# A mixture-of-experts kernel: a small chunk's sums move to another PSUM bank, its gates are made later, and the gathered additions get a second rate

## The chip, the cores and the metric

The kernel runs on one core of one Trainium2 chip. The metric is the device time of one execution in microseconds (us), median over the runs. Within the core five engines run side by side, each with its own instruction stream and held together by semaphores: PE (TensorE, matmuls and weight loads), DVE (VectorE), ACT (ScalarE), POOL (GpSimd) and SP (SyncE, which here only issues DMAs).

## What is computed

x has 2 x 1024 rows of 256 values, all in float32. `xn` is x with its rows normalised.

```python
s = group_norm(tanh(relu(rope(xn @ W_Q)) + hh_b)), turned per batch     # the branch
idx, w = top 6 of 32 experts for each row (within the best 4 of 8 groups of experts)
moe    = sum over the 6 experts: w * (relu(xn @ W1[e].T) ** 2) @ W2[e].T
shared = (relu(xn @ Ws1.T) ** 2) @ Ws2.T
out = x + s * silu(shared + moe)
```

## The kernel before, in words

The 2048 rows are 16 tiles of 128 rows, in four chunks of four tiles. `DENSE = (4, 1, 0, 0)` (line 32) splits them in two kinds. The four tiles of chunk 0 and one tile (number 4) of chunk 1 are *dense*: every one of the 32 experts is computed for all of their rows, and the row's gate (zero where the expert was not chosen) multiplies the hidden values. `BLOCKS` is the list of these two chunks, 0 and 1. The other 11 tiles are *routed*: their rows are sorted by expert into 97 tiles of slots, each slot tile goes through one expert, its results are stored in the table `ytab`, and each row then collects its six results.

The work is a list of 74 units, k = 0 to 73 (`units()`, line 84):

- k = 0 to 7, the early units: the shared experts of all chunks.
- k = 8 to 17: the first ten dense units of chunk 0, one expert over four tiles each.
- k = 18 to 42: the 25 groups of slots, up to four slot tiles each. `LAST` is 42.
- k = 43 to 64: the other 22 dense units of chunk 0.
- k = 65 to 73: the nine dense units of chunk 1. Unit 65 holds the two shared experts of tile 4, each of the other eight holds four experts for that one tile.

Each engine walks the same counter k in program order, and what it does at a k is written out by hand. For a dense unit:

- PE, `first(k)` (lines 951 to 953): the first layer into the bank `hp[k % 2]`; it waits until DVE has read unit k - 2 out of that bank. Then, at the same k, `second_dense(k - 2)` (line 990): the second layer of the unit before last, added up in PSUM over all experts.
- DVE, `relu(k)` (line 1246; line 1248 where there is no gate), then the additions of this k, then `finish` (lines 1273 and 1276) for an output tile that is due.
- ACT, `square(k)` (line 680), later `leave_sum` (line 715), which copies the finished sums out of PSUM at k = 67 for chunk 0 and k = 76 for chunk 1, and `silu_sum` (line 726).
- SP loads the gates of a unit, spread over all partitions, from a table in HBM (`load_gate`, line 471), three units ahead.

PSUM has eight banks: two for `hp`, three for `rot` (turned slot tiles and results of slots, dealt out in turn by the list `uses`, lines 412 to 435), two for `dp`, one for `bp`. Both chunks add up their dense sums in `dp`. So the first `second_dense` of chunk 1, `second_dense(65)` at k = 67, waits for the semaphore `sum_out`, which ACT raises when it has copied chunk 0's sums out, and ACT does that at k = 67 behind `square(67)`.

The additions: from k = 46 (`ADD_AT`) DVE adds the 11 x 6 = 66 gathered pieces, number 0 to 65, to their rows (`add`, line 1265). POOL issues one indirect DMA for each (line 623), in order, at most five ahead of the additions (`AHEAD`, `yk_used`). `adds_by(k)` says how many additions are done by the end of k; with `ADDS = (12, 5)` it grows by 2.4 for each unit:

```python
adds_by = lambda k: max(0, min(NR * K, ADDS[0] * (k - ADD_AT + 1) // ADDS[1]))
```

At k = 65 to 73 these are 3, 2, 2, 3, 2, 3, 2, 2, 2 additions. Output tiles are finished in the order of `FINISH`: tile 12 at k = 66, tiles 0 to 3 at 68 to 71, tiles 13, 14, 15 at 72 to 74 and tile 4 at 77; DVE's part of it stands one k later.

The start of the slots: `one_hot(i)` on DVE (lines 1283 and 1285), `rows_hot(i)` on ACT (line 685) and `place` on PE (line 900) build, routed tile by routed tile (i = 0 to 10), the table of which row stands in which slot. They are laced between the units k = 8 to 14. When all are done DVE writes `ids` (line 1356), and POOL starts the 97 gathers of x (line 614), at most eight ahead of PE, which turns them (`turn_slots`, line 915).

The gates of a dense chunk: `weigh(c)` on DVE (lines 1141 to 1156) normalises the weights and makes a seed for a root; `gate_root(b)` on POOL (lines 580 to 588, 13 instructions for three Newton steps) takes the root; `turn_gates(b)` on PE (line 863) turns the gates; `copy_gates(b)` on ACT (line 670) copies them out; `store_gates(b)` on SP (line 463) stores them and waits until they have landed. For chunk 1 before: `weigh(1)` behind `one_hot(1)`, `gate_root(1)` on POOL between two `low_w` steps (line 569, the low halves of the first-layer weights), and the rest at k = 14 and 15.

Of the kernel before, what the change touches and what calls it, by code (L numbers as in the profile page):

```python
# [6 lines left out]
ACT = mybir.ActivationFunctionType  # L7
# [14 lines left out]
KG, K = 4, 6  # L22
NT = B * T // P
J = 4
NCH = NT // J
# [6 lines left out]
DENSE = (4, 1, 0, 0)  # L32
BLOCKS = [c for c in range(NCH) if DENSE[c]]
# [4 lines left out]
NR = len(ROUTED)  # L38
# [10 lines left out]
GROUPS = (TILES + J - 1) // J  # L49
# [6 lines left out]
POOL_STEPS = 11  # L56
# [6 lines left out]
HRING = 4  # L63
# [3 lines left out]
OHRING = 4  # L67
GRING = 3
LEAD = 10
ADDS = (12, 5)  # L70

W_SCALE = 64.0
WQ_SCALE = 256.0
# [21 lines left out]
def build(nc, x, w1, w2, wr, br, wq, hh_b, gn, cos, sin, consts, out, xtab, ytab, gtab):  # L95
    with ExitStack() as ctx:
# [3 lines left out]
        def bank(name, shape, dt=F32):  # L100
            return ctx.enter_context(nc.psum_tensor(name, shape, dt))
# [12 lines left out]
        w2s = sb("w2s", [P, N, D])  # L114


        acc = xs
# [101 lines left out]
        hf = sb("hf", [P, HRING, CH])  # L219
# [3 lines left out]
        rot = bank("rot", [P, 3, 2, D])  # L223
        dp = bank("dp", [P, 2, 2, D])
        bp = bank("bp", [P, 2, D])
        flat = lambda b: rot[:, b].rearrange("p a d -> p (a d)")
        turned_x = lambda b: flat(b).bitcast(F16).rearrange("p (h k t r) -> p h k t r", h=2, k=KC, t=2)
        turned_words = lambda b: rot[:, b].rearrange("p t (k r) -> p t k r", r=P)
# [11 lines left out]
        gt_stored = sem("gt_stored")  # L240
# [23 lines left out]
        gt_ready = sem("gt_ready")  # L264
# [18 lines left out]
        xt_copied = sem("xt_copied")  # L283
# [5 lines left out]
        shared_out = sem("shared_out")  # L289
# [3 lines left out]
        sum_out = sem("sum_out")  # L293
# [12 lines left out]
        UNITS, EARLY = units()  # L306
        NU = len(UNITS)
        unit_at = {u: k for k, u in enumerate(UNITS)}
# [10 lines left out]
        leaves = {}  # L319
# [8 lines left out]
        store_no = {kh: v for v, kh in enumerate(slot_exits)}  # L328
# [3 lines left out]
        shared_no = {kh: v for v, kh in enumerate(kh for kh in exits if kh not in store_no)}  # L332
        sums = [(c, h) for c in BLOCKS for h in range(len(pairs_of(dense_tiles(c))))]
# [5 lines left out]
        PLACE_AT = HOT_AT + 1  # L339
        HOT_PAIRS = pairs_of(range(NR))  # L340
        PLACED = PLACE_AT + len(HOT_PAIRS)
        GATES_AT = [4, PLACED - 1][0:len(BLOCKS)]


        FIRST_SLOTS = EARLY + LEAD
# [14 lines left out]

        LAST = unit_at[("slots", GROUPS - 1, 0)]
        ADD_AT = LAST + 4
        adds_by = lambda k: max(0, min(NR * K, ADDS[0] * (k - ADD_AT + 1) // ADDS[1]))

        def sums_at(j):

# [35 lines left out]
        def wait_y(engine, v):  # L402
            if exit_by_act(*slot_exits[v]):
                engine.wait_ge(y_act, y_act_before(v + 1))
            else:
                engine.wait_ge(y_out, v + 1 - y_act_before(v + 1))
# [5 lines left out]
        uses = []  # L412
        for k in range(NU + 2):
# [3 lines left out]
            if k + 2 in leaves and UNITS[k + 2][0] == "slots":  # L417
                uses.append(("turn", k + 2, 0))
            uses += [("leave", i, h) for i in leaving(k) for h in range(i != LAST, len(leaves[i]))]
        use_no = {use: n for n, use in enumerate(uses)}  # L420
        bank_of = {use: n % 3 for n, use in enumerate(uses)}

        def wait_bank(engine, *use):

            n = use_no[use]
            if n < 3:
                engine.wait_ge(shared_out, len(shared_no))
                engine.wait_ge(eoff_ready, 1)
                engine.wait_ge(gt_ready, len(BLOCKS))
            else:  # L430
                what, k, h = uses[n - 3]
                if what == "turn":
                    engine.wait_ge(xt_copied, leaves[k][h][-1] + 1)
                else:
                    wait_y(engine, store_no[k, h])

        @block.sync
        def _(sp):
# [111 lines left out]
        def _(pool):  # L550
# [52 lines left out]
            gate_root(0)  # L603
            for s in range(1, POOL_STEPS):
                low_w(s)
                if s == POOL_STEPS - 3:
                    for b in range(1, len(BLOCKS)):
                        gate_root(b)
            pool.wait_ge(ids_ready, 1)
            pool.wait_ge(xtab_stored, 16 * len(ROUTED_CHUNKS))  # L610
            for a in range(TILES):
                if a >= XRING:
                    pool.wait_ge(t_done, a - XRING + 1)
                nc.gpsimd.indirect_dma_start(xg[:, a % XRING, :], None, xtab,  # L614
                                             bass.IndirectOffsetOnAxis(ids[:, a:a + 1], 0))\
                  .then_inc(xg_landed[a % XRING], 16)
            for s in range(YRING):
                pool.wait_ge(y_stored[s], 16 * len(range(s, len(slot_exits), YRING)))
            pool.wait_ge(wlo_dve, WSTEPS - POOL_STEPS)
# [8 lines left out]
        def _(act):  # L628
# [83 lines left out]
            def leave_sum(c):  # L712
                act.wait_ge(sum_done, BLOCKS.index(c) + 1)
                for h, own in enumerate(pairs_of(dense_tiles(c))):
                    nc.scalar.activation(acc[:, own[0]:own[-1] + 1, :], dp[:, h, 0:len(own), :], ACT.Copy)\
                      .then_inc(sum_out, 1)

            def silu_sum(j):
                f = FINISH.index(j)
                if j in ROUTED:  # L720
                    act.wait_ge(yk_used, K * (ROUTED.index(j) + 1))
                else:
                    act.wait_ge(sum_out, 1 + sums.index((j // J, j % J // 2)))
                if f >= 2:
                    act.wait_ge(rows_ready, f - 1)
                nc.scalar.activation(tz[:, f % 2, :], acc[:, j, :], ACT.Silu).then_inc(tz_ready, 1)

            def leave_shared_of(k):
# [97 lines left out]
        def _(pe):  # L826
# [28 lines left out]
            def turn_gates(b):  # L855

                pe.wait_ge(groot_ready, b + 1)
                if b == 0:
                    pe.wait_ge(th_ready, NCH)
                else:  # L860
                    pe.wait_ge(shared_out, len(shared_no))
                for q in range(DENSE[BLOCKS[b]]):
                    mm = nc.tensor.transpose((flat_q, flat(0))[b][0:E, q * P:(q + 1) * P], root[:, q, :], ident)
                mm.then_inc(gt_turned, 1)
# [114 lines left out]
            def second_dense(k):  # L979
                kind, c, u = UNITS[k]  # L980
                pe.wait_ge(squared, k + 1)
                if u == 0 and c != BLOCKS[0]:
                    pe.wait_ge(sum_out, sum(1 for i, h in sums if i < c))
                for n in range(experts_in(c, u)):
                    e = u + n
                    pe.wait_ge(w2_landed[e // W2STEP], 16)
                    for q in range(DENSE[c]):

                        cols = slice((n * DENSE[c] + q) * P, (n * DENSE[c] + q + 1) * P)
                        mm = nc.tensor.matmul(dp[:, q // 2, q % 2, :], hf[:, k % HRING, cols], w2s[:, e, :],  # L990
                                              start=(e == 0 and q % 2 == 0), stop=(e == N - 1), skip_group_check=True)
                if k == last_of[c]:
                    mm.then_inc(sum_done, 1)
# [83 lines left out]
        def _(dve):  # L1077
# [266 lines left out]
            for i in range(NR):  # L1344
                one_hot(i)
                if i % 2 == 1 or i == NR - 1:
                    relu(HOT_AT + i // 2)
                if i == 1:
                    weigh(1)

            dve.wait_ge(one_used, NR)

# [10 lines left out]
            for k in range(HOT_AT + len(HOT_PAIRS), END):  # L1363
# [8 lines left out]
                for s in range(POOL_STEPS, WSTEPS):  # L1372
                    if k == PLACED - 1 + (s - POOL_STEPS) // 2:
                        low_w(s)
                for c in range(2, NCH):
                    if k == WEIGH_AT(c):
                        weigh(c)
                for i in range(0, NR, 2):
# [71 lines left out]
```

## Time and profile before

| | us |
|---|---|
| median of 3 runs | 336.25 |
| the three runs | 336.25, 334.22, 1024.59 |
| the profiled execution, its own time | 335.13 |
| its span, first to last instruction | 333.3 |
| PE busy | 297.5 (89%) |
| DVE busy | 229.0 (69%) |
| ACT busy | 179.3 (54%) |
| POOL busy | 208.0 (62%) |
| mean granted TensorE clock | 0.968 |

All times in rows are microseconds from the first instruction of the profiled execution; 1.83 us of its time lie outside of the span. Busy shares are means over stages with different limits, so what a change in one stage is worth is to be read from that stage. The first views are the page's 40 slices of 8.3 us, for where an engine pauses, and then the chain of waits and the timelines around those pauses.

### The profile page before, as it was taken

The page shows a single profiled execution, that of the slowest core. Times are in us where ns is not written, and L with a number is a line of the kernel's source. Part 1 is how long each engine was busy: PE and PEld are TensorE (multiplying, and loading weights), DVE is VectorE, ACT ScalarE, POOL GpSimd, SP SyncE. Part 2 cuts the span into 40 slices and gives each one's busy share as a digit, 9 for nine tenths or more (in the row PEclk, how much of TensorE's full clock was granted, in tenths as well). Part 3 has the DMA queues.
Part 4 walks back from the last instruction along what each step waited for, and adds up shares of the span by engine and source line. Part 5 has one row for each costly group of instructions (what it writes and reads, how often), then busy time and mean ns, then how long its engine had stood idle before and what let it go on. Part 6 is the DMA issues. An engine that isn't in the chain of part 4 may idle for free.

```text
span 333.3 us, 6927 instructions
## 1 busy us (share of the span) xinstructions
PE 297.5 (89%) x2224; PEld 231.8 (70%) x2224; DVE 229.0 (69%) x585; ACT 179.3 (54%) x293; POOL 208.0 (62%) x226
## 2 busy tenths in 40 slices
PE   0577899879997999999999999998999999995994
PEld 0344666547776977888888698885767767785893
DVE  3788678887631378677778767687767576753774
ACT  3888598695452755557665576653363331212322
POOL 1874656681577777777777777304666777774640
PEclk9997899989997999999999999999999999995999
DMA  7455746722463376676766767555688777666552
GB/s 283 188 176 190 239 146 244 283 94 63 104 180 116 108 222 204 201 204 207 219 203 194 219 196 210 183 173 192 181 327 259 220 197 212 189 182 163 147 154 79
DMA packets 39651, 62.92 MB, mean 189 GB/s; under 512 B 5282, under 2 KB 25538, under 8 KB 39618
## 3 DMA queue, kind: packets, MB, share of 16 engines
q1 hardware_dynamic: 31794, 41.11, 37.2%
q0 software_dynamic: 7824, 21.38, 23.4%
q8 instruction: 20, 0.33, 0.4%
q14 instruction: 13, 0.11, 0.1%
HBM read 46.13 MB, written 16.33 MB: 187 GB/s over the span
## 4 chain that ended last, share of the span: by engine, by line
PE 56%; DMA 15%; POOL 8%; DVE 7%; ACT 6%; issue 6%; DVEq 1%; ACTq 0%
PE rot L962 12%; PE dp L990 10%; DMA yk<-ytab,slot 10%; PE rot L915 5%; PE hp L939 4%; DMA xgt<-xtab,ids 4%; POOL xgt L614 4%; PE hp L951 3%; PE hp L953 3%; PE hp L952 3%; POOL yk L623 3%; PE hp L941 3%; PE hp L940 3%; PE rot L975 2%; DVE xs L1265 2%
## 5 line engine op out<-in xcount | busy, mean ns | idle before, releaser
L614 POOL DMA_INDIRECT xgt<-xtab,ids x97 | 96.4, 994 | 39.7 <-issue 21.3
L680 ACT ACTIVATE hf<-hf 128x512 f32<-128x512 f32 (+2 forms) x74 | 45.8, 619 | 98.7 <-DVE hf L1246 74.8
L623 POOL DMA_INDIRECT yk<-ytab,slot x66 | 64.7, 980 | 44.3 <-DMA ytab<-late 17.1
L990 PE MATMUL dp<-w2s,hf 128*128 128x256 f32 x340 | 83.6, 391 | 4.3 <-issue 4.3
L990 PEld LDWEIGHTS dp<-w2s,hf 128*128 128x128 f32 x340 | 66.1, 198 | 16.2 <-issue 4.7
L694 ACT ACTIVATE xgt<-rot 128x1024 f16<-128x1024 f16 (+1 forms) x49 | 49.3, 1009 | 9.6 <-PE rot L915 9.2
L962 PE MATMUL rot<-w2s,hf 128*128 x194 | 51.3, 391 | 1.1 <-ACT xgt L694 1.0
L953 PE MATMUL hp<-xh,wlo 128*128 128x512 f16 (+2 forms) x148 | 45.0, 322 | 0.0
L952 PE MATMUL hp<-xh,whi 128*128 128x512 f16 (+2 forms) x148 | 45.0, 322 | 0.0
L951 PE MATMUL hp<-xh,whi 128*128 128x512 f16 (+2 forms) x148 | 44.9, 321 | 0.0
L1265 DVE SCALAR_TENSOR_TENSOR xs<-yk,wk,xs 128x256 f32<-128x256 f32 x66 | 32.0, 484 | 16.8 <-DMA yk<-ytab,slot 14.8
L1246 DVE SCALAR_TENSOR_TENSOR hf<-hp,gate_bc 128x512 f32<-128x512 f32 x40 | 27.6, 689 | 20.0 <-PE hp L953 18.4
L939 PE MATMUL hp<-xgt,whi 128*128 128x128 f16 x194 | 38.3, 224 | 1.7 <-issue 1.6
L941 PE MATMUL hp<-xgt,wlo 128*128 128x128 f16 x194 | 37.9, 221 | 0.0
L962 PEld LDWEIGHTS rot<-w2s,hf 128*128 128x128 f32 x194 | 33.3, 190 | 6.5 <-issue 1.9
L940 PE MATMUL hp<-xgt,whi 128*128 128x128 f16 x194 | 37.8, 221 | 0.0
L1248 DVE TENSOR_SCALAR hf<-hp 128x512 f32<-128x512 f32 (+2 forms) x26 | 17.2, 663 | 24.7 <-PE hp L941 22.5
L1258 DVE COPY late<-rot 128x512 f32<-128x512 f32 (+1 forms) x37 | 25.2, 683 | 12.5 <-PE rot L962 12.3
L915 PE MATMUL rot<-cst,xgt 128*128 128x128 f32 x194 | 29.4, 274 | 1.5 <-DMA xgt<-xtab,ids 1.4
L915 PEld LDWEIGHTS rot<-cst,xgt 128*128 128x128 f32 x194 | 23.7, 141 | 6.2 <-DMA xgt<-xtab,ids 2.2
L939 PEld LDWEIGHTS hp<-xgt,whi 128*128 x194 | 18.9, 98 | 6.6 <-issue 3.0
L953 PEld LDWEIGHTS hp<-xh,wlo 128*128 128x128 f16 x148 | 15.3, 103 | 10.4 <-issue 2.0
(162 smaller groups left out, 473.5 us busy)
## 6 DMA issues: line engine op xcount, KB each, us to landing
ytab<-late SPq DMA_DIRECT2D x48, 256.0 KB, 2.8
gate_bc<-gtab SPq DMA_DIRECT2D x40, 256.0 KB, 3.8
late<-in_w SPq DMA_DIRECT2D x17, 256.0 KB, 4.9
w2s<-in_w SPq DMA_DIRECT2D x8, 512.0 KB, 6.4
xs<-in_x SPq DMA_DIRECT2D x4, 512.0 KB, 4.7
xgt<-in_x SPq DMA_DIRECT2D x4, 512.0 KB, 6.5
out<-xgt SPq DMA_DIRECT2D x16, 128.0 KB, 3.7
xgt<-xtab,ids POOLq DMA_INDIRECT x97, 3.3
```

Of the source, the lines that this page charges most:

```text
L614: nc.gpsimd.indirect_dma_start(xg[:, a % XRING, :], None, xtab, bass.IndirectOffsetOnAxis(ids[:, a:a + 1], 0))\
L623: nc.gpsimd.indirect_dma_start(yk[:, n % KRING, :], None, ytab, bass.IndirectOffsetOnAxis(slot[:, n // K, n % K:n % K + 1], 0))\
L694: nc.scalar.activation(xt[:, at:at + len(own), :, :, :].rearrange("p a k h r -> p (a k) h r"), halves(bank_of["turn", k, h])[:, 0:len(own) ...
L915: mm = nc.tensor.transpose(turned_words(bank_of["turn", k, h])[:, q, kc, :], xg[:, a % XRING, kc * P:(kc + 1) * P], ident)
L939: nc.tensor.matmul(o, hi, xt[:, a % TRING, kc, HIGH, :], start=(kc == 0), stop=False)
L940: nc.tensor.matmul(o, hi, xt[:, a % TRING, kc, LOW, :], start=False, stop=False)
L941: mm = nc.tensor.matmul(o, lo, xt[:, a % TRING, kc, HIGH, :], start=False, stop=(kc == KC - 1))
L951: nc.tensor.matmul(o, hi, xh[:, 0, kc, cols], start=(kc == 0), stop=False)
L952: nc.tensor.matmul(o, hi, xh[:, 1, kc, cols], start=False, stop=False)
L953: mm = nc.tensor.matmul(o, lo, xh[:, 0, kc, cols], start=False, stop=(kc == KC - 1))
L962: mm = nc.tensor.matmul(rot[:, bank_of["leave", k, h], q, :], hf[:, k % HRING, s * P:(s + 1) * P], w2_all[:, bass.ds(at[k][s], D)], start= ...
L990: mm = nc.tensor.matmul(dp[:, q // 2, q % 2, :], hf[:, k % HRING, cols], w2s[:, e, :], start=(e == 0 and q % 2 == 0), stop=(e == N - 1), s ...
```

## The change

- `ADDS = (48, 55, 20)`: the additions grow by 48/20 = 2.4 for each unit up to `SECOND` = 65, and by 55/20 = 2.75 for each unit from there. At k = 65 to 73 they are 3, 3, 2, 3, 3, 3, 2, 2, 0.
- Chunk 1's sums are added up in `rot` (bank 0, since it has one tile) in place of `dp`. `second_dense(65)` no longer waits for `sum_out`; it waits until chunk 1's gates are ready and the last user of bank 0 in the list of slots (the result of slot group 23) has been copied out.
- `weigh(1)` goes from behind `one_hot(1)` to k = 20, in the slots.
- `gate_root(1)` goes from between POOL's weight steps to behind its 97 gathers of x.
- `GATES_AT[1]` goes from 14 to 45: `turn_gates(1)` and `copy_gates(1)` run at k = 45, `store_gates(1)` at k = 46.
- The waits of the first three users of `rot` ask for the gates of chunk 0 alone. The first `silu_sum` waits until both gate tables are stored, since their source shares its memory with `tz`.

```diff
-ADDS = (12, 5)
+ADDS = (48, 55, 20)
...
+        sums_of = lambda c: dp if c == BLOCKS[0] else rot
...
-        GATES_AT = [4, PLACED - 1][0:len(BLOCKS)]
+        GATES_AT = [4, EARLY + LEAD + GROUPS + 2][0:len(BLOCKS)]
...
-        adds_by = lambda k: max(0, min(NR * K, ADDS[0] * (k - ADD_AT + 1) // ADDS[1]))
+        SECOND = unit_at[("dense", BLOCKS[1], 0)]
+        adds_by = lambda k: max(0, min(NR * K, (ADDS[0] * (min(k + 1, SECOND) - ADD_AT)
+                                                + ADDS[1] * max(0, k + 1 - SECOND)) // ADDS[2]))
...
+        def wait_left(engine, use):
+            what, k, h = use
+            if what == "turn":
+                engine.wait_ge(xt_copied, leaves[k][h][-1] + 1)
+            else:
+                wait_y(engine, store_no[k, h])
 
         def wait_bank(engine, *use):
...
-                engine.wait_ge(gt_ready, len(BLOCKS))
...
+                engine.wait_ge(gt_ready, 1)
...
             for s in range(1, POOL_STEPS):
                 low_w(s)
-                if s == POOL_STEPS - 3:
-                    for b in range(1, len(BLOCKS)):
-                        gate_root(b)
...
+            for b in range(1, len(BLOCKS)):
+                gate_root(b)
             for s in range(YRING):
                 pool.wait_ge(y_stored[s], 16 * len(range(s, len(slot_exits), YRING)))
...
             def leave_sum(c):
...
-                    nc.scalar.activation(acc[:, own[0]:own[-1] + 1, :], dp[:, h, 0:len(own), :], ACT.Copy)\
+                    nc.scalar.activation(acc[:, own[0]:own[-1] + 1, :], sums_of(c)[:, h, 0:len(own), :], ACT.Copy)\
...
             def silu_sum(j):
...
+                elif f == 0:
+                    act.wait_ge(gt_stored, 16 * len(BLOCKS))
...
             def turn_gates(b):
...
-                    pe.wait_ge(shared_out, len(shared_no))
+                    wait_left(pe, last_user[0])
...
             def second_dense(k):
...
                 if u == 0 and c != BLOCKS[0]:
-                    pe.wait_ge(sum_out, sum(1 for i, h in sums if i < c))
+                    pe.wait_ge(gt_ready, len(BLOCKS))
+                    for b in range(-(-DENSE[c] // 2)):
+                        wait_left(pe, last_user[b])
...
-                        mm = nc.tensor.matmul(dp[:, q // 2, q % 2, :], hf[:, k % HRING, cols], w2s[:, e, :],
+                        mm = nc.tensor.matmul(sums_of(c)[:, q // 2, q % 2, :], hf[:, k % HRING, cols], w2s[:, e, :],
...
             for i in range(NR):
                 one_hot(i)
                 if i % 2 == 1 or i == NR - 1:
                     relu(HOT_AT + i // 2)
-                if i == 1:
-                    weigh(1)
...
-                for c in range(2, NCH):
+                for c in range(1, NCH):
                     if k == WEIGH_AT(c):
                         weigh(c)
```

## Rows read from the trace of the kernel before

**Rows 1.** The page's busy share in tenths, 40 slices of the span: PE and POOL.
```profile
PE   0577899879997999999999999998999999995994
...
POOL 1874656681577777777777777304666777774640
```

**Rows 2.** Timeline of PE, 296 to 304 us: start, duration, line, operation, idle before.
```profile
296.00 1.95 PE L990 MATMUL dp<-w2s,hf 128*128 128x256 f32 x8
297.78 0.22 PE L951 MATMUL hp<-xh,whi 128*128 128x128 f16 x1
...
299.07 0.22 PE L953 MATMUL hp<-xh,wlo 128*128 128x128 f16 x1
303.59 2.05 PE L990 MATMUL dp<-w2s,hf 128*128 128x256 f32 x4 [4.30 <-issue]
```

**Rows 3.** Windows: stretch, busy PE, PEld, DVE, ACT, POOL; then PEclk, DMA share, GB/s.
```profile
299.30:303.60 4.30, 0.01 (x1) 0.04 (x1) 3.36 (x8) 2.54 (x5) 3.38 (x4) 0.75 0.77 180
303.60:308.00 4.40, 4.40 (x29) 3.85 (x29) 0.37 (x1) 0.00 (x0) 1.31 (x2) 0.50 0.51 154
```

**Rows 4.** Timeline of ACT, 300 to 334 us: the two leave_sum.
```profile
302.42 1.07 ACT L715 ACTIVATE xs<-dp 128x512 f32<-128x512 f32 x2
...
329.17 0.38 ACT L715 ACTIVATE xs<-dp 128x256 f32<-128x256 f32 x1 [1.80 <-PE dp L990]
```

**Rows 5.** Timeline of POOL: gathers number 56, 57 and 65 of y.
```profile
304.27 0.95 POOL L623 DMA_INDIRECT yk<-ytab,slot  x1 [0.30 <-issue]
309.59 1.13 POOL L623 DMA_INDIRECT yk<-ytab,slot  x1 [4.37 <-DVE xs L1265]
...
320.01 0.94 POOL L623 DMA_INDIRECT yk<-ytab,slot  x1 [0.30 <-DVE xs L1265]
```

**Rows 6.** The tile yk, 285 to 334 us: from a gather's issue to its landing.
```profile
DMA to landing us min/median/max: 3.1/4.1/5.2
```

**Rows 7.** Timeline of DVE in chunk 1's units: relu(66); a finish and relu(71).
```profile
298.99 0.69 DVE L1246 SCALAR_TENSOR_TENSOR hf<-hp,gate_bc 128x512 f32<-128x512 f32 x1
...
316.97 0.43 DVE L1273 TENSOR_TENSOR xs<-tz,rows 128x256 f32<-128x256 f32 x1 [0.16 <-issue]
...
317.81 0.69 DVE L1246 SCALAR_TENSOR_TENSOR hf<-hp,gate_bc 128x512 f32<-128x512 f32 x1
```

**Rows 8.** Timeline of DVE, 60 to 64 us: weigh(1) starts, then one_hot(2).
```profile
60.04 0.29 DVE L1141 TENSOR_REDUCE wsum<-gate 128x4 f32<-128x128 f32 x1
...
61.61 0.95 DVE L1283 TENSOR_TENSOR xgt<-iota,fb 128x768 f16<-128x768 f16 x1
62.48 1.73 DVE L1285 TENSOR_TENSOR xgt<-iota,fa 128x588 f16<-128x588 f16 x1
```

**Rows 9.** Timeline of ACT at 67 us: the copy of chunk 3's shared sums.
```profile
67.12 1.06 ACT L701 ACTIVATE xs<-rot 128x512 f32<-128x512 f32 x2
```

**Rows 10.** Timeline of PE, 66 to 73 us: place of routed tiles 3 and 4.
```profile
66.75 0.44 PE L900 MATMUL bp<-xgt 128*128 128x98 f16 x6 [0.82 <-ACT xgt L685]
...
71.86 0.44 PE L900 MATMUL bp<-xgt 128*128 128x98 f16 x6 [1.65 <-ACT xgt L685]
```

**Rows 11.** Windows, columns as in rows 3: behind those pauses, and inside the slots.
```profile
72.80:75.50 2.70, 2.70 (x11) 1.23 (x9) 0.71 (x1) 2.07 (x4) 2.56 (x4) 0.50 0.02 4
...
131.20:161.20 30.00, 29.13 (x266) 25.21 (x267) 21.69 (x43) 19.91 (x28) 22.96 (x24) 1.00 0.71 210
```

**Rows 12.** Timeline of POOL: low_w, gate_root(1)'s last, first gathers of x and y.
```profile
62.22 1.35 POOL L569 TENSOR_TENSOR wlo<-late,whi 128x512 f16<-128x512 f32 x1 [2.40 <-ACT whi L654]
...
73.03 0.60 POOL L588 TENSOR_TENSOR eq<-gate,gseed 128x32 f32<-128x32 f32 x1
...
86.18 1.58 POOL L614 DMA_INDIRECT xgt<-xtab,ids  x1 [10.34 <-DVE ids L1356]
...
229.04 1.10 POOL L623 DMA_INDIRECT yk<-ytab,slot  x1 [17.06 <-DMA ytab<-late]
```

**Rows 13.** DMA issues: chunk 1's gate store, KB, us to landing.
```profile
gtab<-tz SPq DMA_DIRECT2D x1, 16.0 KB, 3.5
```

More of the change, by code:

```diff
@@ L419, in build @@
             uses += [("leave", i, h) for i in leaving(k) for h in range(i != LAST, len(leaves[i]))]
-        use_no = {use: n for n, use in enumerate(uses)}
-        bank_of = {use: n % 3 for n, use in enumerate(uses)}
+        bank_of, user_before, last_user = {}, {}, {}
+        for n, use in enumerate(uses):
+            bank_of[use], user_before[use], last_user[n % 3] = n % 3, last_user.get(n % 3), use
+        def wait_left(engine, use):
[4 more added lines that the diff above has]
+                wait_y(engine, store_no[k, h])
         def wait_bank(engine, *use):
-            n = use_no[use]
-            if n < 3:
+            if user_before[use]:
+                wait_left(engine, user_before[use])
+            else:
                 engine.wait_ge(shared_out, len(shared_no))
                 engine.wait_ge(eoff_ready, 1)
-                engine.wait_ge(gt_ready, len(BLOCKS))
[L430 to L435, printed above, removed]
+                engine.wait_ge(gt_ready, 1)
         @block.sync
```

## The prediction

> **What bounds the kernel now.** I read the page's 40 slices first [rows 1]. PE stands at 9 tenths from the tenth slice on, with few exceptions. The last is slice 37 (300 to 308 us), a 5 between nines. POOL is at a steady 7 in the slots and again from slice 32 on, where it gathers y. A gather is about 0.95 us busy and 0.30 us idle, so 7 tenths of busy time is POOL without a pause. Two engines are near their limit, and a stall that goes from one may find the other.
>
> The timeline of PE opens the dip [rows 2]. PE ends `first(67)` at 299.12 and starts `second_dense(65)` only at 303.59, idle 4.30 us. The row names no releaser, but the code has one wait there, `sum_out`. ACT's copy of chunk 0's sums runs from 302.42 to 303.49 [rows 4], and PE starts 0.1 us after it. The copy stands behind `square(67)`, that behind `relu(67)`, that behind the additions of k = 66: a wait for a PSUM bank has tied PE to DVE's additions. The pause costs more than itself. [...]
>
> After that PE runs unbroken until ACT takes chunk 1's sum at 329.17 [rows 4]. From there to the end of the span are 4.13 us (copy, silu, two DVE instructions, one store), which the change leaves as they are.
>
> **The change, part 1: another bank for chunk 1's sums.** `second_dense(65)` can start at 299.12; its new conditions, chunk 1's gates and bank 0 free, are met some 60 us earlier. PE's own work from there is: `second_dense(65)` half of 1.78 us = 0.89; six `first` (68 to 73) at 299.12 - 297.78 = 1.34 us; eight `second_dense` (66 to 73) at 297.78 - 296.00 = 1.78 us [rows 2]. Together 0.89 + 8.04 + 14.24 = 23.2 us, so PE alone would end at 322.3 instead of 329.17: 6.9 us less, 4.5 from the pause and 2.4 from the clock.
>
> I don't think that the rest of the core lets it. What is late next are the additions. In the kernel before, POOL issues gather 56 at 304.27, then stands still for 4.37 us because DVE is stuck behind PE, and issues gathers 57 to 65 from 309.59 to 320.01: 10.42 us for eight steps, 1.30 each [rows 5]. At its shortest a step is 0.95 + 0.30 = 1.25. I take 1.28. Without the pause gather 65 starts at 304.27 + 9 x 1.28 = 315.8. It ends its issue 0.95 us later and lands 4.1 us after that (3.1 to 5.2 [rows 6]), at 320.85.
>
> **Part 2: the new rate.** It adds no work; it moves additions forward. The last two stand at k = 72, ahead of `relu(73)`, no longer behind it. A unit with three additions needs 3 x 1.28 = 3.84 us of gathers, and PE's unit takes 1.34 + 1.78 = 3.12 us. DVE is already late: `relu(66)` runs at 298.99 [rows 7], though PE had ended that first layer near 296.0 [rows 2]. PE tolerates a relu that starts up to about 4.2 us after the end of its `first` (two `second_dense` and a `first`, 4.9, less relu's 0.69). Walking the units with these numbers, an addition never earlier than its gather's landing: relu(67) starts at 302.2, relu(68) at 305.8 (4.2 late, just in time), relu(69) at 308.8, relu(70) at 313.5. PE is free for `first(72)` at 312.7 and waits 1.4 us for relu(70), then some 0.7 us for relu(71).
>
> The end follows from the last gather. Add 65 starts at 320.85 and ends at 321.35; `finish` of tile 3 takes 0.16 + 0.84 = 1.00 (316.97 to 317.81 [rows 7] and the idle before); `relu(73)` 0.69, to 323.05; square 0.63, to 323.7; `second_dense(73)` 1.78, to 325.5. Then the 4.13 us: 329.6 against 333.3, a gain of 3.7 us. The bounds are 6.9 (PE alone decides) and about 1.0: landing at its longest, 1.1 later, and the new pauses dropping the clock in two units, 1.6 more. ACT does its copy of chunk 0 at the same place, beside PE now, and costs nothing.
>
> **Part 3: weigh(1) off the path of `ids`.** `weigh(1)` takes DVE from 60.04 to 61.61, 1.57 us, ahead of one_hot(2) [rows 8]. Here DVE is on the chain. ACT scales what one_hot makes, and PE waits for ACT twice, 0.82 us for tile 3 and 1.65 us for tile 4 [rows 10]; between the two ACT works without a pause. Then PE is unbroken until `place` ends, DVE writes `ids`, and POOL, idle for 10.34 us, starts the gathers of x at 86.18 [rows 12]. So an earlier DVE comes out at the gathers nearly whole. What can swallow some is ACT's copy of the shared sums, since it needs PE's result, which the timeline has ready near 65.7; the copy's two halves start at 67.12 [rows 9], so up to about 1.9 us there is room. I take 1.7 us: the 1.57, and 0.1 from the transpose and copy of chunk 1's gates, which also leave k = 14.
>
> From `ids` on everything moves along. In the slots PE is busy 29.13 of 30 us, and POOL shows 22.96 of 30, gathers back to back [rows 11]; both start earlier by the same amount. [...] I expect pauses of about 1.3 us in place of 2.5, and leave the clock as it is.
>
> The 1.73 us row starts while POOL is inside its `low_w` (62.22 to 63.57 [rows 12]) and ends soon after it. [...]
>
> weigh(1) at k = 20 puts 1.6 us on DVE in the slots, whose relu there has some 4 us of slack: nothing.
>
> **Part 4: gate_root(1), and what goes with it.** On POOL it lasts from 63.57 to 73.63, 10.1 us. Its absence there gives nothing, since POOL then waits 10.34 us for `ids` anyway [rows 12]. Behind the gathers of x it falls into the 17.06 us in which POOL waits for the last y store (211.98 to 229.04): 7 us of cover are left. PE asks for it at k = 45, at about 232. SP's `store_gates` at k = 46 holds SP for its landing, about 3.5 us [rows 13]; queued behind it are one gate load per unit, needed three units (over 9 us) later, and the reloads of x, needed from k = 50. Cost nothing; without cover 3 us. The new wait of the first silu is past by then.
>
> **Sum.** The profiled execution took 335.13 us. 335.13 - 3.7 - 1.7 = 329.7. The median shown, 336.25, stands 1.1 above that execution, and its lowest run 0.9 below.
>
> **Rivals.**
> - *PE alone sets the end.* Gathers land early and DVE keeps up: 335.13 - 6.9 - 1.7 = 326.5. For it: landings down to 3.1 us. Against it: POOL's step cannot go below 1.25, and DVE is 2.7 us late when chunk 1 starts. 0.12.
> - *The clock comes back at the start.* [...] For it: shorter pauses. Against it: they are still over 1 us. 0.13.
> - *Most of it is given back.* [...] 0.23.
> - *Slower: the clock stays low in chunk 1.* [...] At that clock four matmuls of `second_dense` took 1.84 us (303.59 to 305.43) in place of 0.89, and a `first` doubles too, so a unit costs 3.1 us more. The savings of PE's work and of the start are 6.9 + 1.7 = 8.6, so it decides from the third such unit; with five it is 335.13 - 8.6 + 15.6 = 342.1. For it: pauses of 2.5 and 4.3 us dropped the clock here. Against it: it was back within about 4.4 us both times [rows 3, 11], and the pauses I expect are shorter. 0.05.
>
> **How the numbers follow.** The forecast has 0.47, and its own range is 328.4 to 331.6. The range 326.3 to 333.6 leaves out the slower rival, part of the given-back case and a little of the first. Two per cent, about what a measurement of this kernel can tell from no change, is 6.7 us, so faster begins at 328.4. The first two rivals give 0.25 between them, less a little of the second, and the forecast's lower edge adds some: 0.31. Slower: 0.05. The rest, 0.64, is within 2%, though I expect most of it below the time before.
>
> **What would show it.** Right: PE's pause at 299 is gone, and `second_dense(65)` follows `first(67)` at once; POOL has no pause over 1 us from gather 50 to 65; DVE waits for yk in k = 68 to 72, and PE shows one or two pauses of about 1 us late in chunk 1; last matmul about 3.7 us earlier relative to the first y gather. The first gather of x starts near 84.5, the first of y near 227.3. POOL's gate_root stands near 211 with idle time behind it. [...]

## The result, and the profile after

| | before | after |
|---|---|---|
| median (20 runs each), us | 335.83 | 331.83 |
| lowest run, us | 334.19 | 328.21 |
| profiled execution, us | 335.13 | 328.21 |
| its span, us | 333.3 | 326.4 |

The ratio after / before is 0.9861, with a 95% interval of 0.9835 to 0.9886: some 4 us faster, and inside of 2%. Here and below medians are over all runs, while ratios leave out the slow ones, those more than 1.5% above the fastest of their kernel. The forecast was 329.7 with a range of 326.3 to 333.6. The profiled execution of after is the lowest of its 20, so differences between the two profiles (6.9 us) are larger than those between the medians (4.0 us), and what follows keeps the two apart.

The page's slices for after, to be held against [rows 1] (copies at other line numbers: `relu` is L1257, `add` L1276, `second_dense` L1001, `leave_sum` L722):

```profile
PE   0578889989989989999999999998999999999793
...
POOL 1874755430777777777777777333666777777730
...
PEclk9998999999999999999999999999999999999998
```

The 5 of PE in slice 37 is gone; a 7 in slice 38 holds what is left of it. POOL gathers at a steady 7 to slice 38. Its 6, 8, 1 in slices 8 to 10 have become 4, 3, 0 (gate_root(1) gone), and its 3, 0, 4 in slices 26 to 28 have become 3, 3, 3 (gate_root(1) come).

PE in chunk 1 has four short pauses, 3.26 us together, in place of the one of 4.30 us [rows 2]. The timeline of PE, start, duration, what ran, idle before:

```profile
302.80 0.23 PE L960 MATMUL hp<-xh,whi 128*128 128x128 f16 x1 [0.77 <-DVE hf L1257]
...
310.29 0.23 PE L960 MATMUL hp<-xh,whi 128*128 128x128 f16 x1 [1.07 <-DVE hf L1257]
...
317.40 1.99 PE L1001 MATMUL rot<-w2s,hf 128*128 128x256 f32 x8 [0.58 <-ACT hf L687]
...
320.23 1.99 PE L1001 MATMUL rot<-w2s,hf 128*128 128x256 f32 x8 [0.84 <-ACT hf L687]
```

The first two wait for a `relu`, as the forecast had it: `first(70)` for relu(68) and `first(72)` for relu(70). The last two stand in front of the last two `second_dense` and wait for ACT's square, which stands behind relu(72) and relu(73). None of the four drops the clock: it reads 1.00 behind each. The windows of the same stretches, columns as in [rows 3]:

```profile
299.00:303.60 4.60, 3.83 (x46) 3.27 (x44) 2.71 (x6) 1.50 (x4) 3.37 (x5) 1.00 0.61 163
303.60:308.00 4.40, 4.40 (x49) 4.02 (x47) 2.16 (x5) 1.05 (x3) 3.49 (x4) 1.00 0.76 202
72.80:75.50 2.70, 2.70 (x24) 1.89 (x23) 2.70 (x5) 2.28 (x4) 0.00 (x0) 1.00 0.29 95
```

Where [rows 3] had 0.50, behind the pause of 4.30 us, there is 1.00, and it stays 1.00 to PE's last matmul. The third window shows the same for the stretch behind `place` [rows 11], where I had left the clock at 0.50.

The chain of waits at the end names the new bound. Of its last steps these two are gathers, with start, time until landed, and what moved:

```profile
303.44 4.60 DMA yk<-ytab,slot
312.34 4.98 DMA yk<-ytab,slot
```

and DVE's timeline shows what is behind that last landing:

```profile
316.71 1.12 DVE L1276 SCALAR_TENSOR_TENSOR xs<-yk,wk,xs 128x256 f32<-128x256 f32 x2
317.99 0.43 DVE L1284 TENSOR_TENSOR xs<-tz,rows 128x256 f32<-128x256 f32 x1 [0.16 <-issue]
318.49 0.42 DVE L1287 TENSOR_TENSOR xgt<-xs,xgt 128x256 f32<-128x256 f32 x1
318.83 0.68 DVE L1257 SCALAR_TENSOR_TENSOR hf<-hp,gate_bc 128x512 f32<-128x512 f32 x1
```

The last gather (312.34, issue 0.94) lands at 317.3. Its addition, a finish and `relu(73)` follow, and PE's last eight matmuls start at 320.23, after an idle 0.84 us. ACT takes the sum at 322.26.

Cut at events that both kernels have, the two profiles differ as follows. x0 is the first gather of x, y0, y56 and y65 the gathers of y with these numbers, leave is `leave_sum` of chunk 1 (each from the timelines; differences worked out).

| stretch, us | before | after | difference |
|---|---|---|---|
| start to relu(8) | 59.25 | 58.92 | -0.33 |
| relu(8) to x0 | 26.93 | 23.27 | -3.66 |
| x0 to y0 (slots) | 142.86 | 142.43 | -0.43 |
| y0 to y56 | 75.23 | 76.19 | +0.96 |
| y56 to y65 | 15.74 | 11.53 | -4.21 |
| y65 to leave | 9.16 | 9.92 | +0.76 |

The last two rows together, y56 to leave, are 24.90 and 21.45 us, 3.45 less.

### The profile page after: what moved, and what is told of

Its sections match the earlier page's. It is cut to its first block, busy times and chain, and to the rows that moved or that the text cites. A ratio compares the mean times of both kernels' runs of the same rounds, so it can differ in the third digit from the quotient of the medians.

```text
span 326.4 us, 6929 instructions
## 1 busy us (share of the span) xinstructions
PE 293.6 (90%) x2224; PEld 227.7 (70%) x2224; DVE 228.0 (70%) x585; ACT 178.4 (55%) x293; POOL 204.2 (63%) x226
## 4 chain that ended last, share of the span: by engine, by line
PE 46%; DMA 16%; POOL 13%; DVE 9%; issue 7%; ACT 7%; DVEq 2%; ACTq 0%; POOLq 0%
PE rot L971 12%; DMA yk<-ytab,slot 12%; POOL yk L630 7%; POOL xgt L619 5%; PE rot L924 5%; PE dp L1001 4%; PE hp L948 4%; PE hp L950 3%; DMA xgt<-xtab,ids 3%; PE hp L949 3%; PE hp L962 2%; PE hp L961 2%; PE hp L960 2%; PE rot L984 2%; DVE xs L1276 2%
## 5 line engine op out<-in xcount | busy, mean ns | idle before, releaser
L630 POOL DMA_INDIRECT yk<-ytab,slot x66 | 65.9, 999 | 26.9 <-issue 14.3
L1001 PE MATMUL dp<-w2s,hf 128*128 128x256 f32 x272 | 64.9, 381 | 0.0
L1001 PEld LDWEIGHTS dp<-w2s,hf 128*128 128x128 f32 x272 | 51.8, 192 | 9.6 <-issue 0.2
L1276 DVE SCALAR_TENSOR_TENSOR xs<-yk,wk,xs 128x256 f32<-128x256 f32 x66 | 31.9, 484 | 21.1 <-DMA yk<-ytab,slot 18.8
L960 PE MATMUL hp<-xh,whi 128*128 128x512 f16 (+2 forms) x148 | 42.8, 310 | 1.8 <-DVE hf L1257 1.8
L962 PE MATMUL hp<-xh,wlo 128*128 128x512 f16 (+2 forms) x148 | 43.1, 312 | 0.0
L961 PE MATMUL hp<-xh,whi 128*128 128x512 f16 (+2 forms) x148 | 43.1, 311 | 0.0
L1257 DVE SCALAR_TENSOR_TENSOR hf<-hp,gate_bc 128x512 f32<-128x512 f32 x40 | 27.5, 687 | 12.9 <-PE hp L962 12.0
L577 POOL TENSOR_TENSOR wlo<-late,whi 128x512 f16<-128x512 f32 x11 | 16.3, 1485 | 14.5 <-ACT whi L661 14.4
```

The costliest lines, as they stand in the source:

```text
L630: nc.gpsimd.indirect_dma_start(yk[:, n % KRING, :], None, ytab, bass.IndirectOffsetOnAxis(slot[:, n // K, n % K:n % K + 1], 0))\
L960: nc.tensor.matmul(o, hi, xh[:, 0, kc, cols], start=(kc == 0), stop=False)
L961: nc.tensor.matmul(o, hi, xh[:, 1, kc, cols], start=False, stop=False)
L962: mm = nc.tensor.matmul(o, lo, xh[:, 0, kc, cols], start=False, stop=(kc == KC - 1))
L1001: mm = nc.tensor.matmul(sums_of(c)[:, q // 2, q % 2, :], hf[:, k % HRING, cols], w2s[:, e, :], start=(e == 0 and q % 2 == 0), stop=(e == N ...
```

## The experiments

There are twelve entries for nine kernels (d1, d2 and d3 repeat c1, c3 and a4), measured in three batches: the four a; then b1, b2, c1, c3; then b3, d1, d2, d3. Each batch ran on a chip of its own, with runs of the kernel before beside it (medians 335.78, 335.66 and 371.58). All ratios are to the before of the same batch. After itself is in none of them; its ratio is that of the result. Edits are given against after.

### The bank and the rate, taken apart

a1 keeps the bank alone; a2 adds the new rate; a3 is the late weigh(1) and gates alone; a4 is after with the old rate.

```diff
-ADDS = (48, 55, 20)
+ADDS = (48, 48, 20)          # a1, a3, a4
...
-        GATES_AT = [4, EARLY + LEAD + GROUPS + 2][0:len(BLOCKS)]
+        GATES_AT = [4, PLACED - 1][0:len(BLOCKS)]     # a1, a2, with weigh(1) and gate_root(1) at their old places
...
-        sums_of = lambda c: dp if c == BLOCKS[0] else rot
+        sums_of = lambda c: dp                         # a3, with the wait for sum_out
```

> The changed kernel with the start as before (weigh(1) behind one_hot(1), gate_root(1) between the weight steps, gates at k = 14) and the additions at 2.4 a unit throughout: only the sums' bank is new. Theory A (the last gather sets chunk 1's end, and how many additions stand ahead of relu(73) decides what it costs): PE's pause of 4.3 us goes; with two additions behind relu(73) that relu waits for gather 63 and not 65, so the tail gains more than the 3.7 us of the prediction, about 6 (ratio 0.982), and DVE is late by under 3 us at k = 68 to 70. Rival B (the bank frees PE, but the additions at the old rate then pile up behind the units and cost what they save): 2 to 3 us (0.992). x gathers start near 86 in both.

> The changed kernel with the start as before: bank and new rate of additions, nothing of the start. The prediction's tail: 3.7 us less than before (ratio 0.989). Theory A: slower than the same kernel at the old rate by 1 to 2.6 us, since relu(69) to relu(73) wait for gathers that land at 3.84 us a unit where PE needs 3.12. Rival B: faster than the old rate by 1 us or more.

> The changed kernel with both chunks' sums in dp and the wait for sum_out as before, additions at 2.4 a unit: only weigh(1), gate_root(1) and the gates' turning are moved. Theory A: x gathers start 1.7 us earlier (84.5) where the clock still drops near 70 us, 4.0 earlier (82.2) where it does not, as in the profile of the changed kernel; in the median 2 to 3 us (ratio 0.992). Rival C (the start's gain is lost in the slots, where PE and POOL are both full): ratio 0.998 to 1.000 with the x gathers early all the same. PE's pause of 4.3 us near 295 stays.

> The changed kernel with the additions at 2.4 a unit throughout (48, 48, 20), all else as changed. Theory A: no pause of PE in chunk 1, relu(73) waits for gather 63; 1 to 2.5 us faster than the changed kernel (ratio 0.980 against 0.986). Rival B (the new rate is worth its place: additions left behind the last unit lengthen the end): 1 us or more slower than the changed kernel (0.989).

| | median, us (runs) | ratio, 95% | PE's pauses in chunk 1 | y65 to leave | y56 to leave |
|---|---|---|---|---|---|
| a1 | 329.91 (6) | 0.982, 0.9769 to 0.9871 | 0.16, 0.31, 0.93 | 7.23 | 18.80 |
| a2 | 334.42 (12) | 0.9954, 0.992 to 0.9987 | 1.16, 0.46, 0.66 | 9.56 | 21.22 |
| a3 | 334.30 (6) | none given | 4.29 | 9.16 | 24.33 |
| a4 | 328.42 (6) | 0.9768, 0.9719 to 0.9818 | none | 6.57 | 18.40 |

The bank is worth 5.9 us when nothing else is changed (a1, 6 expected), and PE's pause of 4.3 us stays where the sums stay in `dp` (a3). a3's median says little: its six runs go from 327.86 to 337.22. The new rate costs: 4.5 us from a1 to a2, where 1 to 2.6 were expected, and 3.4 us from a4 to after. In both pairs the intervals don't touch, and a1 and a2 are of one batch. a2 also holds the forecast's tail alone, and gave 1.4 us in the median where 3.7 (ratio 0.989) was expected. a4's DVE shows why the rate costs:

```profile
317.26 0.43 DVE L1284 TENSOR_TENSOR xs<-tz,rows 128x256 f32<-128x256 f32 x1 [0.16 <-ACT tz L735]
317.76 0.42 DVE L1287 TENSOR_TENSOR xgt<-xs,xgt 128x256 f32<-128x256 f32 x1
318.11 0.68 DVE L1257 SCALAR_TENSOR_TENSOR hf<-hp,gate_bc 128x512 f32<-128x512 f32 x1
318.71 1.05 DVE L1276 SCALAR_TENSOR_TENSOR xs<-yk,wk,xs 128x256 f32<-128x256 f32 x2
```

In a4 the last two additions stand behind `relu(73)`, in the time in which PE works off its last units. In after they stand ahead of it. So `relu(73)` in after waits for gather 65, and in a4 for gather 63. a4's gather 65 is issued at 314.97, 2.63 us later than after's, yet its `relu(73)` starts 0.72 us earlier and its sum leaves 0.72 us earlier. PE's and ACT's timelines of a4 at the end:

```profile
315.90 5.60 PE L1001 MATMUL rot<-w2s,hf 128*128 128x256 f32 x24
```
```profile
321.54 0.38 ACT L722 ACTIVATE xs<-rot 128x256 f32<-128x256 f32 x1 [0.18 <-PE rot L1001]
```

PE runs without a gap into the copy: in a4 it is PE alone that sets the end. In the other three profiles with the old rate and the new bank PE still waits before its last eight matmuls: 0.93 us in a1, 0.69 in c1, 1.08 in c3. a1's chain has a gather behind that wait, and it is number 63, issued 2.65 us before number 65 (317.71). Its step of the chain, and then PE's timeline:

```profile
315.06 4.94 DMA yk<-ytab,slot
```
```profile
322.91 1.99 PE L1002 MATMUL rot<-w2s,hf 128*128 128x256 f32 x8 [0.93 <-ACT hf L688]
```

y65 to leave averages 9.6 us over the four profiles with the new rate on the first two chips (after, a2, b1, b2) and 6.9 over the four with the old rate and the new bank (a1, a4, c1, c3), while the gathers y56 to y65 take about the same in all eight (11.5 to 11.8). Two gathers' steps, 2 x 1.28 = 2.6 us, are of the same size. No kernel moves the last two additions alone, with the rate otherwise left, so that these two are what costs rests on the traces. They place 2.7 of the 3.4 to 4.5 us; the rest is not placed, since single profiles scatter by 2 to 3 us in the slots alone where the code there is the same (143.2 and 146.2 in a1 and a2, 142.4 and 145.0 in after and a4).

### The start

b1 puts weigh(1) back behind `one_hot(1)` and leaves gate_root(1) behind the gathers of x.

```diff
                 one_hot(i)
                 if i % 2 == 1 or i == NR - 1:
                     relu(HOT_AT + i // 2)
+                if i == 1:
+                    weigh(1)
...
-                for c in range(1, NCH):
+                for c in range(2, NCH):
```

> The changed kernel with weigh(1) back behind one_hot(1) on DVE; gate_root(1) stays behind the gathers of x, the rate stays new. Theory A (DVE's 1.57 us and the clock are the start's gain, POOL's part of it is nothing): from relu(8) to the first gather of x 26.9 us as before, in place of 23.3, with the granted clock back at 0.84 from 66 to 76 us; no pause of PE on ACT's slot copies near 116; time between the bank-and-rate kernel and the changed one, 333 to 334 (ratio 0.993). [...]

The median was 334.72 (10 runs), ratio 0.9885 (0.9836 to 0.9933). The median is 2.9 us above after's, but the ratio is only 0.8 us worse and its interval covers nearly all of after's, so the times don't tell b1 from after. The profile does: relu(8) to x0 took 25.02 us, between before's 26.93 and after's 23.27. Neither expectation fits: Theory A had 26.9 with the low clock, and the 25.0 is the edge of its rival (Rival D), in which POOL's instructions beside DVE were what cost: 25 us or less. DVE's part is 1.75 (b1 to after), and 1.91 came with something else (before to b1). Before's granted clock reads 0.87, 0.50 and 0.77 in the three windows of 2 us from 71.25 to 77.25, and 1.00 in b1's; at full clock the same work would have taken 1.7 us less, so the 1.91 is nearly all clock. Counted from relu(8), b1's long pause ends 0.12 us earlier than that of before, which is all that POOL's absence can have saved DVE and ACT up to there. PE's pauses in b1 are those of before, the granted clock is not.

```profile
69.49 0.44 PE L909 MATMUL bp<-xgt 128*128 128x98 f16 x6 [0.71 <-ACT xgt L692]
74.61 0.44 PE L909 MATMUL bp<-xgt 128*128 128x98 f16 x6 [1.65 <-ACT xgt L692]
75.28 0.44 PE L909 MATMUL bp<-xgt 128*128 128x98 f16 x6 [0.23 <-ACT xgt L692]
```
```profile
72.00:76.00 4.00, 2.12 (x20) 1.28 (x18) 4.00 (x5) 3.93 (x8) 2.92 (x2) 1.00 0.29 103
76.00:80.00 4.00, 4.00 (x30) 2.85 (x29) 4.00 (x6) 3.21 (x6) 0.00 (x0) 1.00 0.20 40
```

Against it a1, whose start is that of before, at the same pause (71.91, idle 1.65):

```profile
72.00:76.00 4.00, 3.77 (x20) 2.07 (x21) 1.83 (x3) 2.92 (x5) 3.61 (x5) 0.59 0.17 40
```

The pause of 1.65 us came with half clock in before, a1 and a2 (0.50 from 73.4 to 75.4 us), and with full clock in b1 (1.00). In the profiles with the whole new start (after, a3, a4, b2, c1, c3) the pauses are 0.78 and 0.23 and the clock is full (1.00 from 70 to 78 us). What decides in b1 I can't say: its stretch lies 2.9 us later, and POOL's gate_root is gone from it; no run separates the two.

### The place of weigh(1), and gate_root(1)

c1 and c3 are a4 with weigh(1), or all three, at k = 17; d3, d1 and d2 are a4, c1 and c3 once more, in one batch. b2 doubles gate_root(1) (six Newton steps in place of three, 25 instructions; its output differs only by rounding). b3 puts it between gathers 79 and 80 of x.

```diff
-        WEIGH_AT = lambda c: PLACED + 4 + c
+        WEIGH_AT = lambda c: FIRST_SLOTS - 1 if c == 1 else PLACED + 4 + c    # c1, d1
+        WEIGH_AT = lambda c: FIRST_SLOTS - 1                                  # c3, d2
...
-                for _ in range(NEWTON):
+                for _ in range(NEWTON * (b + 1)):                             # b2
...
+                if a == 79:                                                   # b3
+                    for b in range(1, len(BLOCKS)):
+                        gate_root(b)
```

> The changed kernel at the old rate, with weigh(1) at k = 17, where DVE stands idle for 7 to 8 us before the first slots, in place of k = 20. Theory E (weigh(1) at k = 20 holds up group_mean(0), ACT's square of it, and ACT's copies of slots behind that, so that PE pauses 0.8 to 1.2 us): that pause on ACT near 116 to 121 us goes, ACT's wait for DVE before its first branch square falls from 3.6 to under 2 us; 1 to 1.5 us faster than the same kernel with weigh(1) at k = 20 (327.2 against 328.4). Rival: the slots are paced by POOL's gathers and take the same 143 to 145 us; no difference.

> As c1, but all three weigh at k = 17 and none in the slots. Theory E: no pause of PE on ACT's slot copies up to 130 us; another 0.5 to 1.5 us faster than c1, unless POOL's gathers pace the slots by then, in which case the same as c1 within 0.5. The clock at the first slots stays at 0.86 to 0.90 in both.

> The kernel c1 once more (rate 2.4 throughout, weigh(1) at k = 17), more rounds, beside d2 and d3 on the same chip. Theory E (weigh(1) at k = 20 holds up group_mean(0), so the branch's square and the slot copies, so PE): d1 is 0.8 us (0.3 to 1.5) below d3, and PE has at most one pause in front of a slot copy of under 0.5 us. Rival H (the pauses on the slot copies are made up by the rings further on): d1 and d3 differ by less than 0.3 us. Both: d1 about 327.5 to 328.5, ratio to before about 0.976.

> The kernel c3 once more (all three weigh at k = 17), more rounds. Theory E says no more than d1's time, 327.5 to 328.5; c3's median of 330.6 was scatter between runs. Rival H2 (three weigh in one unit hold DVE for 4.7 us and relu(17) and the first turns behind them late, in ways that one profile didn't show): 330 to 331 again, 2 to 3 us above d1.

> The kernel a4 once more (everything of the change, but 2.4 additions for each unit to the end), more rounds: 328 to 329 and a ratio of 0.977 (0.974 to 0.980) if the rate is what costs the changed kernel its 3.4 us; 330 or more if a4's median was scatter.

| | median, us (runs) | ratio, 95% |
|---|---|---|
| c1 | 327.63 (6) | 0.9763, 0.9714 to 0.9812 |
| c3 | 330.60 (6) | 0.9864, 0.9818 to 0.991 |
| d1 (as c1) | 366.35 (6) | 0.9888, 0.9826 to 0.9949 |
| d2 (as c3) | 366.87 (6) | 0.9882, 0.981 to 0.9953 |
| d3 (as a4) | 365.88 (6) | 0.9863, 0.9785 to 0.994 |

In a4 weigh(1) at k = 20 delays DVE's group_mean(0); ACT's square for the branch waits for it (3.63 us in after, 1.88 in before), the copies of the turned slots stand behind that square, and PE waits for the copies. PE's timelines of a4, and then of c1:

```profile
118.35 1.13 PE L971 MATMUL rot<-w2s,hf 128*128 x4 [1.21 <-ACT xgt L701]
...
128.99 1.13 PE L971 MATMUL rot<-w2s,hf 128*128 x4 [0.98 <-ACT xgt L701]
```
```profile
128.16 1.13 PE L971 MATMUL rot<-w2s,hf 128*128 x4 [0.32 <-ACT xgt L701]
```

The two pauses shrink to the one of 0.32, as expected, but the time doesn't follow. c1 lies 0.8 us below a4, in different batches; in the one batch that holds both, d1 lies 0.5 above d3. d1's profile does not have what was expected of it: it has pauses of 0.65 and 1.55 us that wait for slot copies. Theory E has c1's wait right and its price at nothing that these runs can tell. c3's 3 us above c1 (same batch, intervals apart) did not come back in d2.

All three of the last batch missed in absolute time: its chip took 371.58 us for the kernel before and some 366 for these, and spent 168.3 to 168.8 us from x0 to y0, where the others spent 142 to 146. The ratios missed too: d3 gave 0.9863 where a4's 0.977 was expected, and d1 0.9888 where 0.976 was. Part of the time can be seen. After x0, d3's PE stands still 14 times in the middle of its work, 10.6 us together, with no wait that the profile shows; a4's does so 3 times, 1.7 us. PE in d3:

```profile
329.05 0.27 PE L960 MATMUL hp<-xh,whi 128*128 128x128 f16 x1 [1.03 <-issue]
```

I have not found the reason. After did not run in that batch, so the rate's cost rests on the first two chips, and nothing shows it on the third.

> The changed kernel with twice the Newton steps for chunk 1's gates (25 POOL instructions behind the gathers in place of 13), output the same but for rounding. In the changed kernel's profile the second of the 13 starts 8.1 us after the first, and 4.1 us are left before the first gather of y. If that pause is there once and the rest takes 0.4 us an instruction: 4.8 us more work, the first gather of y 0.5 to 1 us later, time up by as much. If the pause comes again, or waits for something that ends at a set time: 4 to 8 us later. If there is cover after all (the prediction's 7 us): no difference.

332.17 (10 runs), ratio 0.9915 (0.9872 to 0.9959), 0.3 us above after in the median and 1.8 by the ratios, whose intervals overlap: no difference to be told. The cover was all but used up, though. POOL's timeline of after, the last gather of x, gate_root's first two instructions and its last, and y0, against [rows 12]:

```profile
206.29 0.95 POOL L619 DMA_INDIRECT xgt<-xtab,ids  x1 [0.30 <-issue]
207.26 0.26 POOL L588 TENSOR_TENSOR gwork<-gseed,gate 128x32 f32<-128x32 f32 x1
215.61 0.25 POOL L590 TENSOR_TENSOR gwork<-gwork,gseed 128x32 f32<-128x32 f32 x1 [8.09 <-issue]
...
220.22 0.25 POOL L596 TENSOR_TENSOR eq<-gate,gseed 128x32 f32<-128x32 f32 x1
224.62 1.14 POOL L630 DMA_INDIRECT yk<-ytab,slot  x1 [4.14 <-DMA ytab<-late]
```

Of the 13.2 us 8.09 are a stand behind the first instruction; without it the step would last 5.1. 4.14 us of cover are left. In b2 the doubled root ends at 227.49 and y0 follows 0.56 us later, with no wait for the store: the cover is gone.

> Kernel after with gate_root(1) inside the gathers of x, after gather 79 of 97, in place of behind gather 97. Theory F (the 8.09 us stand after gate_root's first instruction is the price of going from indirect gathers to a tensor operation on POOL, wherever that is done): the same pause of about 8.1 us shows inside the slots, POOL cannot start the next gather of x for 8.1 + 13 x 0.4 = about 13 us, the gathers are at most eight ahead of PE so PE's turns wait, and the stretch from the first x gather to the first y gather (142.4 in after) grows by 6 to 13 us: time 335 to 344. Rival G (the pause is a wait for the last gathers to land or for the table, and is peculiar to the end of the slots): the pause is shorter than 5 us here and the slots grow by less than 3 us, time 329 to 334.

b3 ran in the batch of d1 to d3: 379.02 (2 runs), ratio 1.0234 (1.0125 to 1.0343), 13.1 us above d3. d3 has the old rate and b3 the new one, so the 13.1 are not the root's place alone; the slots, whose code is otherwise the same, are the fairer measure. POOL and then PE:

```profile
204.02 0.26 POOL L588 TENSOR_TENSOR gwork<-gseed,gate 128x32 f32<-128x32 f32 x1
210.98 0.25 POOL L590 TENSOR_TENSOR gwork<-gwork,gseed 128x32 f32<-128x32 f32 x1 [6.70 <-issue]
```
```profile
219.47 0.41 PE L925 MATMUL rot<-cst,xgt 128*128 128x128 f32 x2 [4.14 <-DMA xgt<-xtab,ids]
220.60 0.69 PE L925 MATMUL rot<-cst,xgt 128*128 128x128 f32 x2 [0.72 <-DMA xgt<-xtab,ids]
```

The stand comes along into the middle of the gathers, at 6.70 us, so it belongs to the step from gathers to gate_root and not to the end of the slots (Theory F, a little below its 8.1). The slots took 179.7 us against d3's 168.8, 10.9 more, inside the 6 to 13 expected; the absolute time missed for the same reason as above.

## Why the prediction was right, and where it was not

**The whole.** 329.7 was forecast and 331.83 measured, "within 2%" as the likeliest case, and the mechanism of chunk 1 came out as forecast: the pause gone, PE waiting about 1 us twice for a relu (for relu(68) and relu(70), where relu(70) and relu(71) were forecast), the last gather as the end's bound, copy and store behind it unchanged. The sum came out better than its terms. In the medians the tail alone gave 1.4 us (a2) and not 3.7, the start 2.6 (a2 to after, in different batches) and not 1.7. The two misses partly cancel, and that part of the sum's nearness is luck. With 331.83 the result stands between the forecast case and the rival "most of it is given back", which I had put at 332 to 334 with a tail that gives only 1 to 3 us.

**Part 1, the end of chunk 1.** Nine gathers from y56 to y65 at 1.28 us each: 11.52 forecast, 11.53 in the profile. Landing 4.1, found 4.0 for the last (the chain's 4.98 less 0.94). From y65 to leave 9.67, found 9.92. y56 itself came 0.96 us later after y0, which the forecast did not have, within the scatter of y0 to y56 (75.0 to 77.3 over all profiles of the first two chips). So the tail gave 2.5 us in the profile counted from y0, and 3.45 counted from y56, against 3.7.

**Part 2, the new rate: the step that failed.** "It adds no work; it moves additions forward" was true, and I priced the bank and the rate together. I never walked the units with the old rate beside the new bank. That walk needs nothing more than the step of 1.28 us per gather: with the last two additions behind `relu(73)`, the relu needs gather 63, and 2 x 1.28 = 2.6 us come off the chain. The tail's 3.7 becomes 6.3, close to the 6.9 of PE alone. From y56 to leave the profiles have just that: 24.90 us before, 21.45 after and 18.40 in a4, which is 3.45 and 6.5 less. In the medians the rate cost 3.4 and 4.5 us. The rival "PE alone sets the end" comes true with the old rate in a4, and within about 1 us in a1, c1 and c3; the new rate rules it out.

**Part 3, the start.** 1.7 us was forecast, 3.66 found in the profile. The 1.57 of DVE measured 1.75 (b1 against after). The other 1.91 is the clock but for 0.12: the rival "the clock comes back at the start", with its 1.6 (my estimate from the 2.7 us at 0.50 of [rows 11] and a little beyond), came true in the profile, but its reason (shorter pauses) is not shown, since b1 kept its clock (1.00) with the long pauses (0.71 and 1.65). The long instruction on DVE moved. In before it is the second of `one_hot(2)`, 1.73 us, and it starts beside POOL's `low_w` [rows 8, 12]. In after it is the second of `one_hot(3)`, 1.73 us beside the `low_w` at 61.88 (1.16 long), where that of `one_hot(2)`, with POOL idle, takes 0.76. DVE's timeline of after:

```profile
60.39 0.76 DVE L1296 TENSOR_TENSOR xgt<-iota,fa 128x588 f16<-128x588 f16 x1
...
61.94 1.73 DVE L1296 TENSOR_TENSOR xgt<-iota,fa 128x588 f16<-128x588 f16 x1
```

It comes again at `one_hot(6)`, beside the last `low_w` (67.27): 1.35 and 1.72 us in place of 0.94 and 0.76. What makes DVE take longer beside a `low_w` no run isolates. No pause of PE follows, so it did not land on the chain.

In the medians the start is worth less than in the profiles: 1.5 us (a4 to a1, and a3 to its before for what a3's scatter allows), 2.6 (after to a2). "weigh(1) at k = 20 ... nothing" was wrong as to the wait (two pauses on slot copies of 0.42 and 0.81 us in after, 1.21 and 0.98 in a4) and, as far as the runs tell, right as to the time. Where the other 1 to 2 us of the start's 3.66 go stays open. One thing that I saw and did not settle: between 26 and 54 us, before any instruction that the change moves, the granted clock falls at other places from one kernel to the next. In windows of 4 us it is 0.50 at 30 to 34 us in before and full from 38 on; b1 and a3 have 0.57 there and fall again, to 0.78 at 38 to 46 and 0.57 at 50 to 54. Their relu(8) starts at 62.1 and 62.2, that of the other kernels on the first two chips at 58.9 to 60.3.

**Part 4, gate_root.** The place and the idle time behind it were right, the cover was 4.14 us in place of 7: the 10.1 us of before were a length beside a busy DVE, its last instruction 0.60 [rows 12], where most take 0.25 alone, and in their place came a stand of 8.09 us that no row of before could show. Its cost was nothing, as forecast.

**Best version.** The change with the old rate: a4 at 0.9768, c1 at 0.9763, against after's 0.9861, with intervals that end below that of after. Between the two nothing is told apart. On the third chip the same two kernels gave 0.9863 (d3) and 0.9888 (d1): still faster than before, but whether they beat after there is not shown.

## What to carry to other kernels

When a change moves the place of a wait and also the order of work behind it, walk the last few units once with each alone: which transfer stands ahead of the last relu mattered more here (2.7 us where the traces place it, 3.4 to 4.5 in the medians) than the work that was moved at the start (1.5 to 2.6). What waits for a transfer belongs behind the last instruction that feeds the bottleneck engine, not ahead of it. And single profiles of this kernel differ by several us in stretches where the code is the same, so a gain is read from the medians and its place from the profile.

## What the runs showed of the hardware that I had not expected

- GpSimd, going from indirect gathers to its first drained tensor instruction, stands still behind that instruction: 8.1 us in all ten profiles that have it at the end of the gathers, on three chips, and 6.70 in the middle of the gathers (b3). The profile shows no instruction and no wait in that time, and no run here isolates what it is.
- The same pause of PE (1.65 us) was followed by a granted clock of 0.59 in a1 (72 to 76 us) and of 1.00 in b1 (72 to 80 us).
- One chip, in the one batch that ran there, took 371.58 us for the kernel that took 335.7 on two others. One kernel profiled on two chips (a4 and, on the odd one, d3) places the difference from the first gather of x on: relu(8) to x0 took 23.28 and 23.29 us, x0 to y0 145.0 and 168.8.
